# A graph kernel's VectorE work laid out one piece per tile, row matmuls in tiles 4 to 16, windows of 112 nodes in place of 128

## The reference

```python
inv_dx = 1.0 / jnp.maximum(edge_attr_2[:, 0], 1e-6)
diff = (x[dst] - x[src]) * inv_dx[:, None]
d1 = segment_sum(diff, dst) - segment_sum(diff, src)
S = segment_sum(edge_attr_2[:, 1] * inv_dx, dst)          # the same for each channel
u = x - clip(dt, 0.01, 2.0) * (x * d1 + g * S)
x = layernorm(x + u)
x = layernorm(x + segment_sum(edge_attr_16, dst) / max(counts(dst), 1))
```

## Time and profile before

| | |
|---|---|
| median of 3 runs | 4688.31 us (4681.98 to 4691.01) |
| the profiled execution | 4681.29 us, its span 4679.5 us |
| granted TensorE clock, mean | 0.996 |
| TensorE busy | 4485.3 us (96%), 31379 matmuls |
| VectorE busy | 3823.7 us (82%) |
| ScalarE busy | 1430.6 us (31%) |
| GpSimd busy | 3597.0 us (77%) |
| DMA queues | 9.3% and 6.2% of 16 engines |

### The profile page before, as it was taken

The page is one execution under the profiler, slowest core; times in us unless marked ns, Lnnn a source line. Parts: engine busy times, 40 slices in busy tenths (PEclk is TensorE's granted clock), DMA queues, the critical chain, the costliest instruction groups (busy, mean ns, idle before and its releaser), DMA issues. The chain is left out here.

```text
span 4679.5 us, 90558 instructions
## 1 busy us (share of the span) xinstructions
PE 4485.3 (96%) x31379; PEld 2683.7 (57%) x31380; DVE 3823.7 (82%) x8582; ACT 1430.6 (31%) x1014; POOL 3597.0 (77%) x3133
## 2 busy tenths in 40 slices
PE   3999999999999999999999999999999999999996
PEld 2666555555555555555555555555555555555554
DVE  6888888878888788888888888887888878888886
ACT  4332233222332223322332223322332223322220
POOL 7777777777777777777777777777777777777770
PEclk9999999999999999999999999999999999999998
DMA  3111111111111111111111111111111111111110
GB/s 91 34 34 43 34 33 34 40 37 34 33 34 41 36 34 33 34 43 34 34 34 34 43 34 34 33 42 34 34 34 34 43 34 34 34 34 42 34 22 7
DMA packets 212186, 168.11 MB, mean 36 GB/s; under 512 B 126538, under 2 KB 195662, under 8 KB 211912
## 3 DMA queue, kind: packets, MB, share of 16 engines
q1 hardware_dynamic: 111734, 139.99, 9.3%
q0 software_dynamic: 100000, 25.80, 6.2%
q10 hardware_dynamic: 428, 2.01, 0.1%
HBM read 164.74 MB, written 2.81 MB: 36 GB/s over the span
## 5 line engine op out<-in xcount | busy, mean ns | idle before, releaser
L584 PE MATMUL ps_src<-hi_hot,spread 128*128 128x391 bf16 x25000 | 4309.4, 329 | 91.4 <-DVE hi_hot L858 91.3
L379 POOL DMA_INDIRECT x_src<-in_x_dram,src_i x3125 | 3592.0, 1149 | 955.9 <-issue 861.2
L584 PEld LDWEIGHTS ps_src<-hi_hot,spread 128*128 128x128 f16 x25000 | 2185.7, 97 | 1659.1 <-DVE hi_hot L858 199.4
L858 DVE TENSOR_SCALAR hi_hot<-col_h,hi_f,scale 128x1564 bf16<-128x1564 f16 x3125 | 2127.4, 697 | 205.9 <-PE ps_src L584 205.8
L790 DVE TENSOR_TENSOR spread<-lo_rows,halves 128x640 f16<-128x640 f16 x1250 | 554.4, 485 | 82.1 <-issue 80.0
L525 PE MATMUL ps_x<-xwin,node_of_dst 128*128 128x48 bf16 x3125 | 575.0, 187 | 11.5 <-ACT node_of_dst L467 11.5
L442 ACT CAST parts<-pay 128x425 bf16<-128x425 f32 x125 | 72.5, 580 | 1642.5 <-DVE pay L750 1642.5
L525 PEld LDWEIGHTS ps_x<-xwin,node_of_dst 128*128 128x128 bf16 x3125 | 298.9, 97 | 228.7 <-issue 12.2
L457 ACT CAST parts<-left 128x400 bf16<-128x400 f32 x125 | 71.6, 573 | 1041.2 <-DVE left L847 1041.2
L465 ACT ACTIVATE node_of_dst<-rel_all,row_neg 128x3200 bf16<-128x3200 f16 x125 | 369.8, 2959 | 6.6 <-DMA rel_all<-rel_d 6.6
L467 ACT ACTIVATE node_of_dst<-node_of_dst,ones 128x3200 bf16<-128x3200 bf16 x125 | 370.3, 2963 | 4.1
(11 more groups left out here) (110 smaller groups left out, 1006.1 us busy)
## 6 DMA issues: line engine op xcount, KB each, us to landing
rel_all<-rel_d SPq DMA_DIRECT2D x125, 800.0 KB
x_src<-in_x_dram,src_i POOLq DMA_INDIRECT x3125
a<-in_edge_attr_dram SPq DMA_DIRECT2D x125, 200.0 KB
a<-in_edge_attr_dram SPq DMA_DIRECT2D x125, 25.0 KB, 1.8
src_i<-in_src_dram SPq DMA_DIRECT2D x125, 12.5 KB, 1.6
dst_i<-in_dst_dram SPq DMA_DIRECT2D x125, 12.5 KB, 1.7
xwin<-xparts_d SPq DMA_DIRECT2D x125, 12.0 KB, 1.7
dst_sum<-in_dst_dram SPq DMA_DIRECT2D x1, 1562.5 KB
```

The source lines that it names most:

```text
L379: nc.gpsimd.indirect_dma_start(x_src[:, b, j * F:(j + 1) * F], None, x[:, :], bass.IndirectOffsetOnAxis(ap=src_i[:, b, j:j + 1], axis=0)). ...
L584: last = nc.tensor.matmul(ps_src[:, q, 0:HB], spread[:, b, j, k, :, :].rearrange("p l f -> p (l f)"), hi_hot[:, slot(b, j), q * HB:(q + 1) ...
L858: v.tensor_scalar(hi_hot[:, slot(b, j), :], col_h[:, :], hi_f[:, b, j:j + 1], scale[:, b, j:j + 1], ALU.is_equal, ALU.mult).then_inc(hi_ho ...
```

## The change

WIN goes from 128 to 112: the one-hot `dst_of_node`, the window sums, the windows of x and their one-hots use 112 nodes (partitions, where nodes lie there). The number of further windows is a division by 112, done as a shift by 4, a multiplication by 9363 and a shift by 16. SUM_AT goes from 7 to 11, ROWS_AT from 8 to 4. PIECES is laid out anew: dst_rel and the five dst_hot in tiles 1 to 5, diff in tile 5 in place of 1 and what follows it four tiles later, the ten spread in tiles 12 to 21 in place of two each in tiles 8 to 12, slope in 22, window and attr_left in 23, attr_parts in 24.

```diff
--- before.py
+++ after.py
@@ -22,7 +22,7 @@
     HI = -(-NODES // LO)
     HB = -(-HI // 4)
     HCOL = 4 * HB
-    WIN = 128
+    WIN = 112
     SPL = 3
     HLV = 2
 
@@ -35,7 +35,7 @@
     FULLH = NODES // LO // P
     RING = 10
 
-    assert NODES <= 1 << 14
+    assert NODES <= 1 << 14 and WIN == 16 * 7
     EPS = 1e-5
 
 
@@ -259,10 +259,11 @@
 
 
 
-        SUM_AT, ROWS_AT = 7, 8
-        PIECES = {0: ["x_of_dst"], 1: ["diff"], 2: ["pay"], 3: ["scale"], 4: ["scaled"], 5: ["left"], 6: ["parts"],
-                  8: ["spread"] * 2, 9: ["spread"] * 2, 10: ["spread"] * 2, 11: ["spread"] * 2, 12: ["spread"] * 2,
-                  13: ["dst_rel"], 14: ["dst_hot"] * 2, 15: ["dst_hot"] * 2, 16: ["dst_hot", "slope"], 17: ["window"], 19: ["attr_left"], 21: ["attr_parts"]}
+        SUM_AT, ROWS_AT = 11, 4
+        PIECES = {0: ["x_of_dst"], 1: ["dst_rel", "dst_hot"], 2: ["dst_hot"], 3: ["dst_hot"], 4: ["dst_hot"], 5: ["dst_hot", "diff"],
+                  6: ["pay"], 7: ["scale"], 8: ["scaled"], 9: ["left"], 10: ["parts"],
+                  12: ["spread"], 13: ["spread"], 14: ["spread"], 15: ["spread"], 16: ["spread"], 17: ["spread"], 18: ["spread"],
+                  19: ["spread"], 20: ["spread"], 21: ["spread"], 22: ["slope"], 23: ["window", "attr_left"], 24: ["attr_parts"]}
         FIRST_HALF = ["dst_rel", "dst_hot", "slope", "attr_left", "attr_parts"]
         FIVES = J // 5
         A_STEPS, B_STEPS = 3 + FIVES, 14 + HLV * FIVES
@@ -292,7 +293,7 @@
 
             def load_window(c, b):
                 base = sp.value_load(base_tab[0:1, ds(c, 1)], min_val=0, max_val=NODES - 1)
-                sp.dma_start(xwin[:, b, :], xparts_d[ds(base, WIN), :]).then_inc(win_loaded[b], 16)
+                sp.dma_start(xwin[0:WIN, b, :], xparts_d[ds(base, WIN), :]).then_inc(win_loaded[b], 16)
 
             load_src(0, 0)
             sp.dma_start(dst_all, dst.rearrange("(c e) -> c e", e=CH)).then_inc(dst_all_loaded, 16)
@@ -418,8 +419,8 @@
             def take_turned():
 
                 for q in range(3):
-                    nc.scalar.copy(further_node[:, q * TPB:(q + 1) * TPB, :], turned[:, q * TPB:(q + 1) * TPB, :])
-                return nc.scalar.copy(further_node[:, J - 1, :], turned_last)
+                    nc.scalar.copy(further_node[0:WIN, q * TPB:(q + 1) * TPB, :], turned[0:WIN, q * TPB:(q + 1) * TPB, :])
+                return nc.scalar.copy(further_node[0:WIN, J - 1, :], turned_last[0:WIN, :])
 
             def further_rows(n):
 
@@ -429,7 +430,7 @@
                 def more(g, first):
 
                     act.wait_ge(more_x, g + 1)
-                    act.dma_start(xwin_more[:, :], xparts_d[ds(later(base, g, first), WIN), :]).then_inc(more_loaded, 16)
+                    act.dma_start(xwin_more[0:WIN, :], xparts_d[ds(later(base, g, first), WIN), :]).then_inc(more_loaded, 16)
                     act.wait_ge(more_turned, g + 1)
                     take_turned().then_inc(more_evac, 1)
 
@@ -517,13 +518,13 @@
 
             def turn(hots):
                 for j in range(J):
-                    last = nc.tensor.transpose(turned[:, j, :] if j < 3 * TPB else turned_last, hots[:, j, :], ident_b[:, :])
+                    last = nc.tensor.transpose(turned[0:WIN, j, :] if j < 3 * TPB else turned_last[0:WIN, :], hots[:, j, :], ident_b[:, :])
                 return last
 
             def take_row(nodes, window, j):
 
                 return nc.tensor.matmul(ps_x[:, j // PER, (j % PER) * SPL * F:(j % PER + 1) * SPL * F],
-                                        nodes[:, j, :], window, start=True, stop=True)
+                                        nodes[0:WIN, j, :], window, start=True, stop=True)
 
             def take_rows(nodes, window):
 
@@ -545,7 +546,7 @@
 
                 pe.wait_ge(win_loaded[b], k * 16 + 16)
                 pe.wait_ge(node_hot_ready, m + 1)
-                take_rows(node_of_dst[:, b, :, :], xwin[:, b, :]).then_inc(x_dst_ready, 1)
+                take_rows(node_of_dst[:, b, :, :], xwin[0:WIN, b, :]).then_inc(x_dst_ready, 1)
 
             def further_rows(n):
 
@@ -556,7 +557,7 @@
                     turn(more_node).then_inc(more_turned, 1)
                     pe.wait_ge(more_loaded, g * 16 + 16)
                     pe.wait_ge(more_evac, g + 1)
-                    take_rows(further_node, xwin_more[:, :]).then_inc(more_x, 1)
+                    take_rows(further_node, xwin_more[0:WIN, :]).then_inc(more_x, 1)
 
                 further_in(pe, span, more)
                 return span
@@ -587,7 +588,7 @@
                         last.then_inc(hi_hot_free, 1)
                     r = (j - ROWS_AT) * 2 + q // 2
                     if rows_of is not None and q % 2 and 0 <= r < J:
-                        one = take_row(node_of_dst[:, rows_of, :, :], xwin[:, rows_of, :], r)
+                        one = take_row(node_of_dst[:, rows_of, :, :], xwin[0:WIN, rows_of, :], r)
                         if r == J - 1:
                             one.then_inc(x_dst_ready, 1)
 
@@ -692,7 +693,12 @@
             step(v.tensor_tensor(more_i[0:C, 0:1], lim[0:C, 1:2], lim[0:C, 0:1], ALU.subtract))
             step(v.tensor_scalar(base_diag[0:C, 0:C], ident[0:C, 0:C], lim[0:C, 0:1], None, ALU.mult))
             settle()
-            step(v.tensor_single_scalar(more_i[0:C, 1:2], more_i[0:C, 0:1], 7, ALU.arith_shift_right))
+
+            step(v.tensor_single_scalar(more_i[0:C, 1:2], more_i[0:C, 0:1], 4, ALU.arith_shift_right))
+            settle()
+            step(v.tensor_single_scalar(more_i[0:C, 0:1], more_i[0:C, 1:2], 9363, ALU.mult))
+            settle()
+            step(v.tensor_single_scalar(more_i[0:C, 1:2], more_i[0:C, 0:1], 16, ALU.arith_shift_right))
             settle()
             v.tensor_copy(more_f[0:C, :], more_i[0:C, 1:2]).then_inc(tab_sum, 1)
             dve.wait_ge(tab_sum, 2)
```

## The result

The changed kernel takes 4549.62 us (median of 6 runs, 4548.90 to 4550.23) against 4689.33 for the kernel before: a ratio of 0.9702, 95% interval 0.969 to 0.9715. It is 3% faster; 5080 us, 8% slower, was forecast. Its profiled execution took 4549.4 us, with a span of 4547.5.

What follows compares the result with a forecast made beforehand. Gathers were taken to bound the kernel: 122 chunks paying 3.25 us each add 396 us, less 5 us of tail, giving 5072 us profiled and 5080 us median (+8.4%). The range of 8 in 10 was 4700 to 5200 us.

Steps and rivals of the forecast that it cites:

- What bounds the kernel: Whole span before the change: gathers set the pace, 36.4 us a chunk; TensorE alone would need 35.4 us a stage.
- That a hot holds a gather, and what a gather costs from diff to parts: VectorE's src one-hots (hots) block gathers, stretching 0.94 us to 1.58 or 2.40; diff-to-parts sequence stays as before.
- the seven gathers that were to keep their times: First seven gathers behind the landing that starts diff: times stay 3.40 to 13.28, as before.
- One gather per 2.00 us, and it locks: Spread stretch: with one piece behind each hot, each gather waits through to the next hot's end, every 2.00 us.
- the walk through the spread stretch: Gather starts stepped through the stage, spread from 14.52 at 2.00 us steps; whole cycle 39.75 us a chunk.
- The dst stretch: Five dst one-hots, one behind each hot: same pattern as spread, gathers at 31.45, 32.90, 34.80.
- only hots hold a gather: Rival: a tensor_tensor does not block gathers; 34.4 us a chunk, TensorE bound, about 4565 us, -2.6%; chance 0.19.
- The window: TensorE's window sum with 112 columns for 128: saves under 0.17 us a stage, hidden while TensorE starves.
- The row matmuls: Row matmuls from tile 4: their condition is signalled at 35.7, TensorE reaches tile 4 near 40, so hidden.
- The tail: Kernel end: with diff in tile 5, TensorE is further along when the last gather lands, 5 us less.
- The wait figures: VectorE's wait for gathered rows grows from 340.6 to about 1000 us, TensorE's for hots from 91 to about 500.
- The sign of TensorE as the bound: If GpSimd gets real waits on hi_hot_free, TensorE has become the bound.

Runs made afterwards that it cites:

- e4: The kernel before with only one gather of five issued: 4562.29 us, ratio 0.9725 to the kernel before.
- e16: The kernel before with one spread piece per tile and windows of 112, otherwise in the old order: 4544.97 us, ratio 0.9673 to the kernel before.
- e1: The changed kernel with windows of 128 again: 4566.33 us, ratio 0.9734 to the kernel before.
- e3: The changed kernel with two spread pieces per tile again, in tiles 12 to 16: 4618.32 us, ratio 0.9846 to the kernel before.
- e13: The kernel before with only its ten spread pieces one per tile, later pieces moved back: 4562.35 us, ratio 0.9739 to the kernel before.
- e2: The kernel before with windows of 112 and nothing else: 4741.01 us, ratio 1.0113 to the kernel before.
- e14: The changed kernel with SUM_AT 7 and ROWS_AT 8 as before: 4583.02 us, ratio 0.9783 to the kernel before.
- e8: The changed kernel with the two inputs of each spread piece exchanged: 5325.41 us beside 5081.03 for the kernel before, on a chip with TensorE pauses.
- e9: The changed kernel with the two inputs of each dst one-hot exchanged: 5320.76 us beside 5081.03 for the kernel before, on a chip with TensorE pauses.

## Why the prediction was wrong

*What bounds the kernel*: right. Gathers set the pace (e4), TensorE's own need is 35.4 us (35.39 in e4, 35.28 after).

*That a hot holds a gather, and what a gather costs from diff to parts*: right in the main. The same 1.58 and 2.40 us came back at 2027.71 and 2029.59. Of the seven gathers that were to keep their times the last five did; in place of the first two stands one of 2.10 us at 2022.80.

*"One gather per 2.00 us, and it locks"*: this step, in the walk through the spread stretch, failed, and with it the sum. The lock exists, as e16 shows, for gathers that start 0.20 us into a hot. But the walk took every start inside a hot with a piece behind it as held, and the traces do not bear that out (table above). The stretch's first gather, 14.52 in the walk, started 0.12 us into its hot, where gathers get through: it took 0.95 us in place of 1.83. The next started at 0.33 and took 1.16 us. From then on the gathers stay ahead of the hots, and the hots are the ones lengthened. The stretch's gathers cost 0.95 us instead of 1.70, which makes 35.24 us a chunk in place of 39.75.

Behind this stand two assumptions. One was that where gather and hot meet the gather waits. The trace of before already had the other case, which I did not weigh; in its timelines of VectorE and GpSimd stand

```profile
2025.80 0.88 DVE L858 TENSOR_SCALAR hi_hot<-col_h,hi_f,scale 128x1564 bf16<-128x1564 f16 x1
```

```profile
2025.35 0.94 POOL L379 DMA_INDIRECT x_src<-in_x_dram,src_i  x1 [0.30 <-issue]
```

a gather of 0.94 us, and over it a hot of 0.88 in place of 0.68. Who started first does not decide it either: the gather of 16.03 started 0.19 us before its hot and was the one held. Counted over six traces (before, changed, e1, e3, e13, e16), of the gathers that start with no hot under way: where a hot starts 0.15 to 0.40 us later, the gather is held and the hot is not (2349 gathers, medians 1.10 to 1.20 us); where it starts 0.45 to 0.55 us later, the gather takes 0.94 us and the hot 0.80 us or more (249). The second assumption was that any tensor_tensor behind a hot keeps a waiting gather out. I had this from `scaled`, `halves`, `parts` and the dst one-hots, and carried it to the spread pieces, though no gather in the trace had started in the first half of a hot with one behind it. The gathers at 2033.55 and 2034.80 show that it does not hold for every start.

*The dst stretch* followed the rule better: 1.50 and 2.10 us at 2020.99 and 2022.80.

*The rival "only hots hold a gather"* gave 4557 to 4565 us with 34.4 us a chunk and TensorE as the bound. Its time was near and its bound right, but by luck: its mechanism was not. The gathers of 2.40 us at 2029.59 and 2.10 at 2022.80 last until a second hot is over, which by that rule they would not have met, so tensor_tensors are still in the way; and what opened the spread stretch was VectorE standing back. The Trainium skill's "SBUF — State Buffer", Who interferes with whom, says that of a VectorE operation in a two-port mode and GpSimd whoever issues first gets the shared ports for the whole instruction. The trace agrees in part only: the hot of 2036.72, which starts 0.45 us after a gather of 0.95 us, is lengthened by 0.21 us only, less than the 0.50 us that the gather still lasts, and the gather of 2033.55 gets through a hot that started before it.

*The window*, costed at under 0.17 us a stage and hidden: the size was right (0.134), the cover was not there, since TensorE had become the bound; and alone it costs 51 us, which no term had. *The row matmuls*: hidden, as said. *The tail*, 5 us less, was worked out for a kernel that ends with its gathers, and this one does not. *The wait figures* (1000 and 500 us) fell with the cycle. *The sign of TensorE as the bound*, real waits of GpSimd on `hi_hot_free`, failed too: its longest wait for TensorE is 0.3 us, as before, though TensorE is the bound; e4 has such waits.

## What to carry to other kernels

Where GpSimd issues indirect DMAs back to back, read its durations before its busy share: 77% busy with pauses of one fixed length is an engine that never waits. Then lay its instructions over VectorE's and look at both for ones that take longer than their least: each tells who was held. Slack on VectorE can be given away by the order of its pieces; here one short piece in place of two between the long ones did it. And take such a lock apart by an experiment before forecasting with it: pieces shorter by 35 ns (e2) moved this kernel by 1%, and whether a gather starts 0.12 or 0.20 us into a hot decides between 0.95 and 1.70 us. A forecast of a lock needs its times to better than that, or a range that holds both outcomes.

## What the runs showed that was not expected

- A hot that starts some 0.45 us after a gather is lengthened from 0.68 to 0.89 us, and the spread piece behind it from 0.48 to 0.52, tile after tile; one that starts 0.15 to 0.40 us after it holds the gather.
- The lock at 2.00 us steps that the forecast named exists: it stands in some stages of e16, the fastest version.
- Less work on VectorE (windows of 112 alone) made the kernel 1.1% slower.
- One program took 4551 or 4614 us in runs beside each other (e14).
- On two of the five chips of these experiments TensorE paused in each stage of the kernels with all gathers, and its clock fell behind such a pause. The kernel before itself took 5081 and 4924 us there; the changed kernel was 4.7% slower than it on the second, and on the first two variants of it (e8, e9) were. On the other three chips the changed kernel or its variants repeat the gain (0.9712 and 0.9682 for the kernel itself). The 3% is the result on chips without these pauses.
